# Attention's first convolution: one of a unit's four row combinations computed on VectorE instead of GpSimd

## The reference

```python
def _mdta(x, w_qkv, b_qkv, w_dw, b_dw, temperature, w_out, b_out):
    qkv = conv(x, w_qkv, 1x1) + b_qkv
    qkv = conv(qkv, w_dw, 3x3, depthwise, SAME) + b_dw
    q, k, v = split(qkv, 3)                 # per head: channels x pixels
    q, k = q / norm(q), k / norm(k)
    attn = softmax(einsum('bhcn,bhdn->bhcd', q, k) * temperature)
    out = einsum('bhcd,bhdn->bhcn', attn, v)
    return conv(out, w_out, 1x1) + b_out

x = x + _mdta(_gn(x), ...)
x = x + _L1_conv_ref(_gn(x))                # the second block
```

## Time and profile before

| | us |
|---|---|
| three runs | 1527.93, 1524.94, 1519.10 |
| their median | 1524.94 |
| the profiled execution | 1521.04 |
| its span, first to last instruction | 1519.0 |

### The profile page before, as it was taken

One profiled execution on the slowest core, in us unless ns is written; L12 is line 12 of the kernel. 1 busy time (PEld: TensorE's weight loads), 2 busy tenths in 40 slices (PEclk: granted clock), 3 DMA queues, 4 the chain that ended last, 5 costly groups with the idle time before them and its releaser, 6 DMA issues. The chain is left out here.

```text
span 1519.0 us, 33952 instructions
## 1 busy us (share of the span) xinstructions
PE 1312.3 (86%) x13569; PEld 1055.0 (69%) x13569; DVE 1147.2 (76%) x1911; ACT 873.1 (57%) x946; POOL 647.7 (43%) x676
## 2 busy tenths in 40 slices
PE   0699998987899499999958888999959976999998
PEld 0699897986899255555538878879949973555554
DVE  8577677468863599999936666764786847999998
ACT  1455564211552499999925555532125517999996
POOL 3698894332320253442037777833422203354400
PEclk9999999997999699999969999999989987999999
DMA  6366631693132445364245676416703315463533
GB/s 232 84 203 202 199 109 52 188 282 120 54 135 118 170 139 143 90 183 88 66 131 165 206 215 181 118 41 192 199 2 144 150 43 190 124 174 97 160 75 100
DMA packets 80002, 211.27 MB, mean 139 GB/s; under 512 B 15761, under 2 KB 19955, under 8 KB 77187
## 3 DMA queue, kind: packets, MB, share of 16 engines
q1 hardware_dynamic: 65956, 159.38, 34.1%
q0 software_dynamic: 6720, 36.93, 9.1%
q10 hardware_dynamic: 7168, 12.78, 3.0%
HBM read 92.54 MB, written 67.04 MB: 105 GB/s over the span
## 5 line engine op out<-in xcount | busy, mean ns | idle before, releaser
L1687 PE MATMUL acc<-rnd,ident 128*128 128x376 f32 x1152 | 391.8, 483 | 24.3 <-ACT rnd L1668 24.3
L1687 PEld LDWEIGHTS acc<-rnd,ident 128*128 128x128 f32 x1152 | 216.5, 192 | 145.1 <-ACT rnd L1668 25.7
L888 PE MATMUL ps_a<-wa,xa 128*128 128x192 f16 x1536 | 301.4, 249 | 2.2 <-DMA xc<-low 2.0
L888 PE MATMUL ps_a<-wb,xb 128*128 128x192 f16 x1536 | 300.4, 249 | 0.0
L1520 DVE TENSOR_TENSOR prod<-fc,near 128x1504 f32<-128x1504 f32 x144 | 247.2, 1717 | 33.2 <-DMA near<-f_planes,index 16.9
L1663 ACT ACTIVATE rnd_m<-prod,plus_round,scale 128x1504 f32<-128x1504 f32 x144 | 235.8, 1637 | 62.1 <-DVE prod L1520 51.5
L550 POOL TENSOR_TENSOR vt<-z 96x256 f32<-96x256 f32 x248 | 248.8, 1024 | 18.7 <-ACT z L792 18.6
L1629 DVE SCALAR_TENSOR_TENSOR over<-prod,scale,rnd 128x1504 bf16<-128x1504 f32 x144 | 255.4, 1776 | 0.0
L1575 POOL DMA_INDIRECT near<-f_planes,index x56 | 156.5, 2795 | 212.1 <-DVE prod L1520 204.4
L1668 ACT ACTIVATE rnd<-rnd_m,minus_round 128x1504 f32<-128x1504 f32 x144 | 223.2, 1550 | 4.7
L888 PE MATMUL ps_a<-wfa,xa 128*128 128x96 f16 x1536 | 157.9, 206 | 4.5 <-issue 4.1
(11 more groups left out here) (305 smaller groups left out, 2350.6 us busy)
## 6 DMA issues: line engine op xcount, KB each, us to landing
xb<-xa ACTq DMA_DIRECT2D x64, 195.0 KB, 2.7
f_planes<-img SPq DMA_DIRECT2D x8, 1536.0 KB, 14.1
fc<-f_planes SPq DMA_DIRECT2D x16, 768.0 KB, 5.3
v_a<-xa SPq DMA_DIRECT2D x40, 260.0 KB, 2.6
v_b<-xb SPq DMA_DIRECT2D x40, 260.0 KB, 3.1
xa<-v_a SPq DMA_DIRECT2D x40, 260.0 KB, 4.6
xb<-v_b SPq DMA_DIRECT2D x40, 260.0 KB, 5.3
near<-near SPq DMA_DIRECT2D x96, 107.9 KB, 2.2
```

What stands on the lines that cost most here:

```text
L888: mm = lambda a, w, first, end: nc.tensor.matmul(out(i), a, w, start=first, stop=end)
L1687: nc.tensor.matmul(o(m), k["ident"][:, :], rnd[:, n % RNDS, BR * m:BR * m + BR, :], start=False, stop=False, skip_group_check=True)
```

## The change

Combination 0 of every unit from 1 on is computed by a new VectorE function, `outer_term`; GpSimd's `v_terms` makes combinations 1 to 3. GpSimd's halves become (1, 2) after an even pair's sum and (3) after an odd one's. VectorE calls `outer_term(1)` after `first_terms`, `outer_term(u+2)` after each of the first three low parts, and `outer_term(u+5)` at the end of unit u in the loop, so behind `qk_low(2u+1)` and ahead of `rows_out(2u+2)`. `v0_made` now counts units whose combination 0 is done, and `high` and `norm` wait for it beside `v_made`.

```diff
--- before.py
+++ after.py
@@ -538,7 +538,7 @@
 
                 at, out = 4 * (u % 4), vt[:, u % 2].rearrange("p (j i) x -> p i j x", i=4)
                 row = lambda d: z[:, at + d:at + d + 3:2, :]
-                if 0 in which:
+                if 1 in which:
                     if u == UNITS - 1:
                         nc.gpsimd.memset(z[:, at + 5, :], 0.0).then_inc(padded, 1)
                         pool.wait_ge(padded, 2)
@@ -560,11 +560,11 @@
 
             pool.wait_ge(padded, 1)
             for u in range(1, AHEAD + 1):
-                v_terms(u, range(4))
+                v_terms(u, (1, 2, 3))
             for n in range(PAIRS):
                 even_sum(n)
                 if n // 2 + 1 + AHEAD < UNITS:
-                    v_terms(n // 2 + 1 + AHEAD, (0, 1) if n % 2 == 0 else (2, 3))
+                    v_terms(n // 2 + 1 + AHEAD, (1, 2) if n % 2 == 0 else (3,))
 
             for n in range(UNITS - 1):
                 m = lambda j: side[:, n % 2, :, j * C:j * C + C]
@@ -595,6 +595,16 @@
                 for i, (p_, q_, op) in enumerate(V_TERMS):
                     last = nc.vector.tensor_tensor(out[:, i], z[:, p_:p_ + 3:2, :], z[:, q_:q_ + 3:2, :], op)
                 last.then_inc(v0_made, 1)
+
+            def outer_term(u):
+
+                dve.wait_ge(normed, u + 2)
+                if u >= 2:
+                    dve.wait_ge(lo_done, u - 1)
+                p_, q_, op = V_TERMS[0]
+                row = lambda d: z[:, 4 * (u % 4) + d:4 * (u % 4) + d + 3:2, :]
+                nc.vector.tensor_tensor(vt[:, u % 2].rearrange("p (j i) x -> p i j x", i=4)[:, 0], row(p_), row(q_), op
+                                        ).then_inc(v0_made, 1)
 
             def low_part(u):
                 dve.wait_ge(hi_done, u + 1)
@@ -625,8 +635,10 @@
                                         ).then_inc(qk_lo, 1)
 
             first_terms()
+            outer_term(1)
             for u in range(AHEAD):
                 low_part(u)
+                outer_term(u + 2)
             for u in range(UNITS):
                 rows_out(2 * u)
                 qk_low(2 * u)
@@ -634,6 +646,8 @@
                 if u + AHEAD < UNITS:
                     low_part(u + AHEAD)
                 qk_low(2 * u + 1)
+                if u + 2 + AHEAD < UNITS:
+                    outer_term(u + 2 + AHEAD)
 
 
             dve.wait_ge(gram_out, 1)
@@ -774,9 +788,8 @@
             group_stats_root(nc, act, k, ps_s, mom, stat_summed, stat_rooted)
 
             def high(u):
-                if u == 0:
-                    act.wait_ge(v0_made, 1)
-                else:
+                act.wait_ge(v0_made, u + 1)
+                if u > 0:
                     act.wait_ge(v_made, u)
                 if u >= SLOTS:
                     act.wait_ge(conv_done, 4 * (u - SLOTS) + 4)
@@ -796,6 +809,7 @@
                 act.wait_ge(turned, u + 2)
                 if u >= 4:
                     act.wait_ge(v_made, u - 3)
+                    act.wait_ge(v0_made, u - 2)
                 s, at = u % 2, 4 * (u % 4) + 2
                 n = 3 if u == UNITS - 1 else 4
                 if u % 4 == 3 and n == 4:
```

## The result

The changed kernel takes **1544.09 us** (median of four runs, 1541.79 to 1550.24); the kernel before took 1522.02 beside it (four runs, 1513.23 to 1527.93). The ratio is 1.0156, with a 95% interval from 1.0094 to 1.0218: slower, by 22.1 us on the medians. Forecast were 1537.4, 12.5 us slower, with a range of 1518 to 1552. The profiled execution of after is the slowest of its four: 1550.24 us, with a span of 1548.5 (before 1519.0), 29.5 us more.

What follows compares the result with a forecast made beforehand. A loop through three engines, with VectorE and GpSimd hindering each other, was taken as the bound, not TensorE. Mean lap 6.19 to 6.58 us, 32 x 0.39 = +12.5 us on 1524.94, gave 1537.4 us; range 1518 to 1552.

Steps and rivals of the forecast that it cites:

- The loop and the hand-made lap: First convolution: a loop through three engines sets the pace; laps reckoned from the low part's start, 6.44 or 6.98 us.
- GpSimd first: Lap where GpSimd's even sum runs before qk's low half after the low part: 6.98 us, where it was 6.11.
- The price guessed by columns: New VectorE instruction, made to wait, ends 0.28 us after GpSimd's combination, taken between 0.21 and 0.415.
- 20 to 7: Image 0's 27 laps after the low part: VectorE first in 20, GpSimd in 7, assumed unchanged.
- rival 2: After the low part GpSimd always goes first: every lap 6.98 us, +25 us, 1550; chance 0.15.
- the 20 of 27: Argument against GpSimd always first: VectorE led in 20 of 27 laps though GpSimd had asked earlier still.
- lap of 6.44: VectorE first after the low part, GpSimd combinations between its later short instructions: 6.44 us, where it was 6.22.
- the sum: Lap change times 32 laps, image 0's 27 and image 1's last 5: 32 x 0.39 = +12.5 us.
- Rival 1: VectorE keeps its turn from the new instruction to `td`: lap 5.90 us, -9.3 us, 1515.6 on the median; chance 0.20.
- Nothing for the 22 laps of image 1: Image 1's other 22 laps cost nothing, covered by waits for rows and TensorE; without that cover 8.6 us more.
- Waits and start: Added waits of the new instruction, `high` and `norm`, and the kernel's start, all costed at nothing.
- TensorE's floor of 5.80 us: TensorE alone needs 5.80 us a unit: two pairs' convolutions, two grams and one `turn`.

Runs made afterwards that it cites:

- e9_behind: Changed kernel with the new VectorE instruction moved one place on, behind the even pair's `td` and ahead of `y`: 1531.70 us in one run (before 1525.42).
- e4_late: Changed kernel with GpSimd's even sum waiting for the low part's end: 1507.84 us, ratio 0.9936 to the kernel before.
- e7_slot_late: Changed kernel with the new instruction behind the even pair's `y` and the even sum waiting for the low part's end: 1498.89 us, ratio 0.9828 to before.
- e6_alone: Changed kernel with GpSimd again making all four combinations, its combination 0 into an unread spare buffer: 1561.34 us, ratio 1.0232 to before.
- e2_hold: Changed kernel with GpSimd's two even-pair combinations waiting until VectorE has made `td`: 1510.41 us, ratio 0.9931 to before.
- e8_three: Changed kernel with three places in `vt`, so the new instruction waits for a low part one lap old: 1541.96 us in one run (before 1525.42).
- e1_slot: Changed kernel with the new instruction moved into VectorE's idle time behind the even pair's `y`: 1499.93 us, ratio 0.9874 to before.
- e3_both: Changed kernel with the new instruction behind the even pair's `y` and GpSimd's two even-pair combinations held until `td`: 1498.10 us, ratio 0.9867 to before.
- e5_relief: Changed kernel without VectorE's new instruction in the loop, nobody making combination 0 from unit 5 on: 1504.10 us, ratio 0.9865 to before.

## Why the prediction was right, and where its size was off

**The loop and the hand-made lap: right.** For GpSimd first the working gave, from the low part's start: qk's low half over at 2.14, combination 2.73, new one 3.01, second combination 3.60, `td` 3.81, `y` 3.84, lap 6.98. Measured in the lap at 137.68: 2.13, 2.72, 3.005, 3.59, 3.80, 3.84, 6.97. The price guessed by columns, 0.28 beyond the combination, was 3.005 - 2.72 = 0.285.

**The step that failed is who comes next.** The prediction carried over 20 to 7 from before, let GpSimd in behind every short VectorE instruction in the 20 as well, and so took 6.58 as the mean lap. Neither held in the changed kernel. In image 0 and the last five laps of image 1 the share was 0 to 32: rival 2, which had a chance of 0.15. And in the 16 laps of image 1 where VectorE did go first it kept its turn through the new instruction, so no lap of 6.44 occurred. Rival 2's argument, that GpSimd asks ahead of qk's low half, fits the changed kernel but isn't enough, since in e9_behind GpSimd asks as early and went first in 9 laps of 27. The argument against it, "the 20 of 27", came from a kernel in which `td` stood behind qk's low half, and e9_behind shows that with `td` there such a share does come back.

With the share at 0 to 32 the sum gives 32 x 0.79 = +25.3 us; measured are 18.75 + 3.84 = 22.6. The 2.7 between lie in before's laps: four took 6.39 to 7.55 us (6.39 is the lap of the earlier trace rows, reckoned at 6.11), so their mean was 169.87 / 27 = 6.29, not 6.19. That 1544.09 lies inside the forecast's own 1533 to 1545 is in part luck. By its laps the result is rival 2's, whose 1550 came down by these 2.7 and by the 2.9 that before was faster beside the change (1522.02) than in the three runs ahead of it (1524.94).

**Rival 1** is a real sequence, not a fancy: 16 laps of image 1 and all of e4_late. In image 0 of the changed kernel GpSimd asks too early for it.

**Nothing for the 22 laps of image 1: open.** The traces differ there by 5.1 us, inside the 8.6 given as a bound. On the medians the change is 22.1 us slower, which the 22.6 of the other 32 laps make up by themselves; the profiled execution was 6.2 us above its median. That laps of 6.97 make the waits for rows longer, and these bring the lower clock on more often, is a reading of the rows; no run took it apart.

**Waits and start: right at nothing.** ScalarE's wait for combinations fell to 1.2 us, as foretold, and no added wait shows. TensorE's floor of 5.80 us was slightly high: with TensorE never idle, e7_slot_late has a mean lap of 5.76.

## What to carry to other kernels

When an instruction moves from one engine to another and the two hinder each other, what counts is not its 0.41 us but where it stands: add up the alternating chain from the last long instruction to the one that the loop waits for, and put the new one behind that. A large wait of a profile (33.0 us here) can vanish while the kernel gets slower, if its waiter has a later wait in the same loop. An observed share of who goes first belongs to the order in which it was observed; for a new order, bound the sum by both pure cases and give each a real chance.

## What the runs showed of the hardware

The Trainium skill (SBUF — State Buffer, § SBUF: two separate sides) has the one who starts first keep the port pair for its instruction. The runs agree on the lock: behind a combination of GpSimd the new instruction took 0.94 us, not 0.41, and ended 0.285 us after it. They show how the next turn depends on two things. One is when GpSimd asks. In the nine kernels where the even sum is what asks (all but before and e6_alone, 27 laps of each image), it was issued less than 0.15 us before the low part's end, or after it, in 250 laps, and VectorE went first in 249. The other is what VectorE has behind qk's low half. Where the even sum came earlier (0.15 to 0.19 us before the end, nearly all at 0.17 or 0.18), GpSimd went first in 112 of 112 laps with the new instruction there (after, e2_hold, e8_three), and in 40 of 124 with `td` there (e1_slot, e3_both, e5_relief, e9_behind). In the changed kernel some 0.1 us in the asking is so worth a lap of 6.97 or 5.91. A rule by time of arrival alone doesn't give this: in the 84 other laps the even sum was issued ahead of qk's low half and was served behind it. What in the second instruction decides stays open. e8_three excludes the wait on the running low part for who goes first, but with that wait gone VectorE no longer kept its turn through the new instruction (6.45, not 5.91).
